# New orders of the same operations on four engines, with new users of the PSUM banks

## The reference

```
def local_ffn(x):                    # called twice, 2 layers each
    for l in range(2):
        h = shift_token(x)
        q, k, v = split(h @ wqkv[l])           # 8 heads of 64
        q, k = l2norm(q) * qs, l2norm(k) * ks  # then rotary with a scale by position
        o = local_attention(q, k, v)           # windows of 64, each looks at itself and the one before
        x = x + o @ wo[l]
        h = layernorm(shift_token(x)) * g + b
        a, gate = split(h @ w1[l] + b1[l])     # 341 each
        x = x + (a * gelu(gate)) @ w2[l] + b2[l]
    return x
x = x + 0.5 * local_ffn(layernorm(x))
x = x + causal_attention(layernorm(x))         # one head of 128, 1024 x 1024
x = x + 0.5 * local_ffn(layernorm(x))
```

## Time and profile before

| | us |
|---|---|
| median of 3 runs (lowest, highest) | 2623.74 (2619.52, 2624.07) |
| span of the profiled execution | 2623.2 |
| PE busy in it | 2558.0 |
| DVE, ACT, POOL busy | 2376.0, 2346.8, 2056.4 |

### The profile page before, as it was taken

The page is one execution under the profiler, slowest core; times in us unless marked ns, Lnnn a source line. Parts: engine busy times, 40 slices in busy tenths (PEclk is TensorE's granted clock), DMA queues, the critical chain, the costliest instruction groups (busy, mean ns, idle before and its releaser), DMA issues.

```text
span 2623.2 us, 80275 instructions
## 1 busy us (share of the span) xinstructions
PE 2558.0 (98%) x29132; PEld 2063.6 (79%) x29132; DVE 2376.0 (91%) x6206; ACT 2346.8 (89%) x7379; POOL 2056.4 (78%) x2185
## 2 busy tenths in 40 slices
PE   5999999999999999998999999999999999999998
PEld 4778777877788888886997777778777788888876
DVE  7999999999999999996888999999998999999995
ACT  5999999999999999995555999999999999999996
POOL 7999999988887877872104999999988888787873
PEclk8999999999999999999999999999999999999999
DMA  4121111111111111110000111111111111111110
GB/s 105 44 51 31 28 38 31 28 28 39 24 32 28 28 42 26 32 28 8 9 1 11 32 28 32 26 38 32 29 24 39 28 32 40 30 40 36 36 40 26
DMA packets 63810, 83.95 MB, mean 32 GB/s; under 512 B 11538, under 2 KB 30652, under 8 KB 63420
## 3 DMA queue, kind: packets, MB, share of 16 engines
q1 hardware_dynamic: 63420, 78.82, 13.1%
HBM read 11.67 MB, written 4.19 MB: 6 GB/s over the span
## 4 chain that ended last, share of the span: by engine, by line
PE 83%; POOL 6%; DVE 5%; ACT 4%; issue 2%; SPq 0%; DMA 0%; ACTq 0%; POOLq 0%; DVEq 0%
PE PS L678 8%; PE PS L662 8%; PE PS L628 7%; PE PS L652 7%; PE PS L619 6%; PE PS L742 6%; PE PS L621 6%; PE PS L620 6%; PE PS L723 4%; PE PS L725 3%; PE PS L724 3%; PE PS L644 3%; PE PS L690 2%; PE PS L853 2%; PE PS L692 2%
## 5 line engine op out<-in xcount | busy, mean ns | idle before, releaser
L4440 ACT ACTIVATE P<-PS,MX 128x128 f32<-128x128 f32 x2048 | 754.3, 430 | 2.1 <-DVE MX L2248 1.2
L5756 POOL TENSOR_TENSOR T<-T,SQ 128x512 f32<-128x512 f32 x512 | 652.1, 1284 | 115.3 <-DVE SQ L2209 111.7
L5792 POOL TENSOR_TENSOR P<-P,RI 128x512 f32<-128x512 f32 x512 | 527.8, 1042 | 73.8 <-DVE RI L2254 71.7
L4440 ACT ACTIVATION_READ_ACCUMULATOR P<-PS,MX 128x1 f32 x2048 | 535.6, 268 | 0.0
L5769 POOL TENSOR_TENSOR T<-T,RN 128x512 f32<-128x512 f32 x512 | 525.9, 1048 | 6.2 <-DVE RN L2242 3.8
L2190 DVE TENSOR_REDUCE SS<-SQ 128x8 f32<-128x512 f32 x512 | 343.8, 681 | 44.6 <-ACT SQ L4395 37.9
L4395 ACT ACTIVATE SQ<-PS 128x512 f32<-128x512 f32 x512 | 338.1, 662 | 45.9 <-PE PS L621 35.0
L619 PE MATMUL PS<-WH,YH 128*128 128x512 f32 x768 | 346.1, 451 | 6.9 <-POOL YL L5745 3.3
L2248 DVE TENSOR_REDUCE MX<-PS 128x4 f32<-128x512 f32 x512 | 345.8, 678 | 6.5 <-PE PS L652 6.3
L2209 DVE TENSOR_TENSOR SQ<-PS,TAB 128x512 f32<-128x512 f32 x512 | 349.1, 682 | 2.3
L2201 DVE TENSOR_TENSOR T<-PS,TAB 128x512 f32<-128x512 f32 x512 | 344.2, 682 | 7.1 <-PE PS L628 3.3
(11 more groups left out here) (155 smaller groups left out, 5938.4 us busy)
## 6 DMA issues: line engine op xcount, KB each, us to landing
VP<-VP SPq DMA_DIRECT2D x480, 128.0 KB, 2.3
out_dram<-X SPq DMA_DIRECT2D x16, 256.0 KB, 2.6
X<-in_L_attn_x_dram SPq DMA_DIRECT2D x7, 512.0 KB, 4.5
SG<-in_L_ffn_w_dram SPq DMA_DIRECT2D x5, 341.0 KB, 3.0
SG<-in_L_ffn_wqkv_dram SPq DMA_DIRECT2D x4, 384.0 KB, 3.4
SGQ<-in_L_ffn_wqkv_dram SPq DMA_DIRECT2D x4, 256.0 KB, 3.5
X<-in_table_dram SPq DMA_DIRECT2D x2, 512.0 KB, 6.5
P<-in_L_ffn_wo_dram SPq DMA_DIRECT2D x2, 256.0 KB, 3.2
```

What stands on the lines that cost most here:

```text
L4440: ins = act.activation(P[:, g, p, :], PS[:, b, 128 * p:128 * p + 128], ACT.Exp, bias=MX[:, g, p:p + 1], accum_out=SM[:, g, p:p + 1])
L5756: pool.tensor_tensor(T1[:, k, :], T1[:, k, :], SQ[:, (2 * n + 1 - x) % 3, :], ALU.add).then_inc(added[x], 1)
L5792: pool.tensor_tensor(P[:, g], P[:, g], RI[:, g, :].unsqueeze(2).broadcast_to([128, NPAIR, 128]), ALU.mult).then_inc(p_scaled, 1)
```

## The change

No operation is added, removed or changed in shape. All four lists are replaced; the rounds begin at 4 and 36 (before 9 and 41), since the lists before them are now short, and end at 32 and 64. The users of the banks are new, the banks of the attention too. The copies of the next layer's weights stand in calls of their own (`stage_qk`, `stage_v`, `rest_of_qk`, `rest_of_v`) and no longer inside `square`, `split_y`, `rotate_add` and `normalise_qk`. DVE takes the statistics of chunks 64 to 68 during the attention.

```diff
-ROUNDS = {0: (9, 32), 1: (41, 63)}
+ROUNDS = {0: (4, 32), 1: (36, 64)}
 ROTA = [
-    [("W2", 4), ("TK1", 3), ("O0", 4), ("V1", 2), ("TK0", 2), ("S0", 2), ("P2", 3), ("G0", 3)],
-    [("Q0", 2), ("YR", 3), ("TQ0", 2), ("K1", 1), ("O1", 3), ("NR", 1)],
...
+    [("TQ0", 3), ("TK1", 3), ("YT", 4), ("K0", 1), ("TQ0", 2), ("S0", 2), ("G1", 3)],
+    [("S2", 4), ("V1", 3), ("NR", 2), ("Q0", 1), ("TQ1", 2), ("WO", 2)],
...
-A_SCORE, A_TURN, A_OUT, A_IN = (0, 2), (4, 5), 6, 7
+A_SCORE, A_TURN, A_OUT, A_IN = (6, 3), (0, 2), 1, 5
```

The begin of DVE:

```diff
             y0_up(0)
+            ln_stats(2)
+            ln_aggregate(2)
+            ln_eps(2)
+            ln_stats(3)
             y0_up(1)
-            ln_stats(2)
+            ln_aggregate(3)
+            ln_eps(3)
+            ln_stats(4)
             sum_squares(0, 0, K)
```

More of the change, by code:

```diff
@@ L944, in first_steps @@
-            turn_back(0)
+            scores(4, 0)
+            turn_p(3, 1)
             project(5, 1, K)
-            turn(4, 1, K)
-            scores(4, 0)
-            project(5, 1, Q)
-            turn_p(3, 1)
+            turn(4, 1, Q)
+            turn_ln(6)
+            turn_p(3, 2)
+            to_gate(0, 0)
             wo(2)
-            project(5, 0, V)
-            turn(4, 1, Q)
-            turn_p(3, 2)
             turn_p(3, 3)
+            to_gate(0, 1)
             values(3, 0)
@@ L994, in first_steps @@
-            turn(6, 0, K)
-            turn(6, 1, K)
-            project(7, 1, K)
-            scores(6, 0)
-            turn_p(5, 1)
-            wo(4)
-            project(7, 0, V)
-            turn(6, 1, Q)
-            turn_p(5, 2)
-            turn_p(5, 3)
-            values(5, 0)
-            values(5, 1)
-            to_gate(1, 0)
-            to_gate(1, 1)
-            to_gate(1, 2)
-            turn_ln(8)
-            scores(6, 1)
-            wo(5)
-            to_up(1, 0)
-            to_up(1, 1)
@@ L1014, in first_steps @@
-            project(7, 1, V)
-            to_up(1, 2)
-            project(8, 0, K)
-            project(8, 0, Q)
-            down(1)
-            turn(7, 0, Q)
-            turn(7, 0, K)
-            turn_ln(9)
-            turn_p(6, 0)
-            turn_p(6, 1)
-            project(8, 1, K)
-            turn_p(6, 2)
-            turn(7, 1, K)
-            scores(7, 0)
-            turn_p(6, 3)
-            turn_rows(2)
-            turn(7, 1, Q)
-            project(8, 1, Q)
-            values(6, 0)
@@ L1052, in first_steps @@
-            turn_p(7, 3)
-            values(7, 0)
-            values(7, 1)
-            to_gate(2, 0)
-            to_gate(2, 1)
-            to_gate(2, 2)
-            turn_ln(10)
-            scores(8, 1)
-            wo(7)
-            to_up(2, 0)
-            to_up(2, 1)
-            project(9, 1, V)
-            to_up(2, 2)
-            project(10, 0, K)
-            project(10, 0, Q)
-            down(2)
-            turn(9, 0, Q)
-            turn(9, 0, K)
-            turn_ln(11)
-            turn_p(8, 0)
@@ L1146, in first_steps @@
-            wo(10)
-            project(13, 0, V)
-            turn(12, 1, Q)
-            turn_p(11, 2)
-            turn_p(11, 3)
-            values(11, 0)
-            values(11, 1)
-            to_gate(4, 0)
-            to_gate(4, 1)
-            to_gate(4, 2)
-            turn_ln(14)
-            scores(12, 1)
-            wo(11)
-            to_up(4, 0)
-            to_up(4, 1)
-            project(13, 1, V)
-            to_up(4, 2)
-            project(14, 0, K)
-            project(14, 0, Q)
@@ L3264, in into_attention @@
             a_add(0, 2)
+            ln_stats(TURN)
             a_copy_p(0, 4)
@@ new lines, in local @@
+                split_o(t - 5, 1)
+                gelu(s - 4, 1)
+                split_y(t - 2, 0)
+                y0_down(t - 1)
+                gelu(s - 4, 2)
+                round_w1(s - 3)
+                exp_rows(t - 4, 1)
+                square(t - 2, 0, K)
+                copy_v(t - 3, 0)
+                copy_k(t - 3, 0)
+                copy_q(t - 3, 0)
+                split_y(t - 2, 1)
+                square(t - 2, 0, Q)
+                exp_rows(t - 4, 2)
+                exp_rows(t - 4, 3)
@@ L4989, in into_attention, with attention @@
+                y0_down(t)
+                copy_q(t - 2, 1)
+                square(t - 1, 1, Q)
+                stage_qk(s)
+                copy_p(t - 3, 2)
+                copy_p(t - 3, 3)
+                exp_rows(t - 2, 0)
+                gelu(s - 3, 0)
+                split_o(t - 3, 0)
+        def attention():
+            split_o(TURN - 5, 1)
+            gelu(PAIRS - 4, 1)
+            split_y(TURN - 2, 0)
+            gelu(PAIRS - 4, 2)
             exp_rows(TURN - 4, 1)
-            split_o(TURN - 5, 0)
+            square(TURN - 2, 0, K)
+            copy_k(TURN - 3, 0)
@@ new lines, in local @@
+                rest_of_y(t - 2, 0)
+                normalise_qk(t - 3, 0, K)
+                normalise_qk(t - 3, 0, Q)
+                rotate_add(t - 3, 1, Q)
+                rest_of_w1(s - 3)
+                ln_root(t)
+                normalise_qk(t - 3, 1, Q)
+                scale_p(t - 4, 0)
+                normalise_qk(t - 3, 1, K)
+                ln_rows(t)
+                rest_of_y(t - 2, 1)
+                rotate_add(t - 2, 0, K)
+                scale_p(t - 4, 1)
+                row_rstd(s - 3)
```

5077 lines of the change are left out of this document (1447 added, 3630 removed), and 201 rows, old and new, of tables (FIRST_USERS, LAST_USERS, ROTA).

## The result

The changed kernel takes 2675.6 us (median of 4 runs, 2674.12 to 2676.56) against 2623.9 us for the kernel before on the same chip: ratio 1.0201, 95% interval 1.0186 to 1.0215. It is 2% slower, outside the range of 2588 to 2640. The profiled run has a span of 2672.3 us, 49.1 more than before. One execution of one experiment (e13_notab2) ran almost throughout at a low granted clock and took 4190.07 us; it is left out of all comparisons, and that kernel was run again as e16_notab3.

The account below looks back on a forecast made before the run. PE was taken as the limit in the rounds, with DVE, ACT and POOL also nearly full. The terms -3 - 3 - 3 - 1 - 4 - 1 = -15 took 2623.7 to 2609 us, range 2588 to 2640.

Parts of the forecast that it names:

- Neighbours on PE: In the rounds: costs between adjacent PE operations change by -0.05 us a round, -3 us over 60 rounds.
- Waits in the rounds: From a chunk's last projection to its first turn: a quarter of 11 us of first-layer-round waits goes, -3 us.
- the 0.9 us of slack: First-layer rounds: 11.1 us of PE cover less the 10.2 us way from last projection to first turn.
- this term is 0: ACT's order in the rounds: changes between exp and gelu stay at 123, so no cost from table loads, 0.
- Rival A: In the rounds: the shortened way is late at turn(t-3, 0, K), so slower, 2629 to 2650 us; chance 0.20.
- The begin: Before the first down: first turn at about 38 us, gain of -3 us, bounds -12 and +5.
- if it loses the same 17: The begin: first down at 125 us if waits take 17 us as before, 108 if nothing waits.
- break-even: The begin: a first down at 120 us would neither gain nor lose, as 4 us of work moved behind it.
- The clock: In the begin: the idle gap is as long, so the same loss from a lower granted clock, later; 0.
- Into the attention: Before the last values: to_gate and to_up fill 3.2 idle us but were cover behind it; -1 us, between -4 and +3.
- The end: End of the kernel: same exchange of fill and cover round the last values; -1 us, between -4 and +3.
- Out of the attention: After the attention: POOL is the bound, earlier statistics let it start sooner; -4 us, between -7 and 0.

Follow-up runs that it names:

- e13_notab2: Changed kernel without the second layer's tables, four small reduces in their place; ratio 1.0178, one execution at a low granted clock 4190.07 us.
- e16: Changed kernel without the second layer's tables, four small reduces in their place, run again; 2668.61 us, ratio 1.0173.
- e1: Changed kernel with less ACT work in the rounds: copy_p copies only 128 of 512 columns; 2662.28 us, ratio 1.0152.
- e3: Changed kernel with round_w1 moved later on ACT, behind copy_v, and rest_of_w1 behind row_rstd on POOL; 2667.66 us, ratio 1.0175.
- b2: Kernel before with round_w1 moved earlier on ACT, straight behind the last gelu of the pair; 2631.35 us, ratio 1.0026.
- e4: Changed kernel with own banks for Q1 and V0 of the first chunk, in the begin and after the attention; 2674.6 us, ratio 1.0200.
- e14: Changed kernel with own banks for Q1, V0 and also NR of the first chunk, in the begin and after the attention; 2679.04 us, ratio 1.0210.
- e7: Changed kernel with chunk 0's sums and root ahead of later statistics on DVE, and rest_of_y ahead of ln_rows on POOL; 2677.59 us, ratio 1.0202.
- e11: Changed kernel with own banks for Q1 and V0, and the first turn of K ahead of the next chunk's two Q projections; 2681.18 us, ratio 1.0220.
- e9: Changed kernel with the step into the attention back in the old order on PE, ACT and DVE to match; 2677.21 us, ratio 1.0201.
- e17: Changed kernel with two K projections moved behind the last two groups of values of the attention; 2676.12 us, ratio 1.0201.
- e2: Changed kernel with the second gelu ahead of the second split_o in ACT's order of the rounds; 2682.95 us, ratio 1.0232.
- e5: Changed kernel with the second layer's tables built one chunk later and one rotate_cos ahead of a sum_squares on DVE; 2678.01 us, ratio 1.0203.
- e12: Changed kernel with all three to_up ahead of wo on PE, and two gelu earlier on ACT; 2681.19 us, ratio 1.0217.
- e10: Changed kernel with the second layer's four table operations on 64 columns in place of 512; 2676.35 us, ratio 1.0196.
- b1: Kernel before with the second layer's four table operations on 64 columns in place of 512; 2621.25 us, ratio 0.9989.

## Why the prediction was wrong

*Neighbours on PE* (-0.05 us a round, -3, between -0.3 and +0.2 a round). With less work for ACT (e1) a YT round is within 0.05 to 0.14 us of the old one: inside the bounds, not on the side forecast, and not told apart from a rest of the wait.

*Waits in the rounds* (-3). This step failed twice. It took the 0.45 us by which an LT round is longer for waits that could go; but the LT round came out at 36.85 again, so this order won none of it (what it is, no run shows; less work for ACT did not change it either, 36.86 in e1). And it checked one way only, from `project(t - 1, 1, K)` to `turn(t - 3, 0, K)`. That way held: PE has no listed wait there, though the 0.9 us of slack was never measured. What was late was a way I had dismissed with "this term is 0": ACT's list. I had counted its table loads (124 in both kernels) and not whether the 21 us of its work from `copy_p` to the second `gelu` still fit beside PE's work between the same two points. They miss by 0.48 us a round, and only where `turn_ln` isn't there as cover. Rival A had the right kind of cause, at the wrong place and in the wrong rounds.

*The layer boundaries* were not in the sum at all. One conditional step moved from where its wait was already met to behind `gelu(s - 4, 2)`: 7.6 us, by e3, with b2 as its reverse. The rest of the 12.5, 4.9 us, is about the YT rounds' own wait in the same stretch: e1 took 5.9 us off the two boundaries.

*The begin* (-3). The first `turn` came at 37.19 as forecast (38), the first `down` at 129.90 and not 120. The step that failed is "if it loses the same 17": with the 70 us of work that the prediction counts behind the first `turn`, it lost 129.90 - 37.19 - 70 = 22.7. And -3 had been chosen although the sum with the same loss already stood at 125, 5 us over break-even. The list's shorter ways no longer cover a pause of DVE, which is also longer here (7.2 us against 4.5): 5.4 us of the 11.8 (e16). The other 6 us are not settled. They are not the shared banks (e4, e14), nor the order of statistics and sums (e7), nor PE's order round the first `turn` (e11).

*The clock* was put at 0, "the same loss, later". It was not the same: the granted clock's mean over the first 70 us is 0.78 against 0.88, and it fell behind the attention too, where it had not. In the begin its share lies inside the 5.4 and the 6 us above, behind the attention it is 1 to 2 us.

*Into the attention* (-1). The bounds named this loss, up to +3: the groups put ahead of the last `values` had been cover behind them. It was 4.2 us, and that cause is not shown: putting them back (e9) gave nothing sure. ACT's wait of the YT rounds is not in it either, since e1 has 84.4 us here. *The end* (-1): +0.7, inside its bounds.

*Out of the attention* (-4). The term took POOL for the bound. POOL was relieved for the first 20 us as forecast, and nothing was gained: PE waited 4.03 us for DVE to free bank 2. Of the 9.4 us the banks explain 1 and the clock 1 to 2; e17 and e11 excluded the position of two projections and of the first turn. Some 6 us stay open.

Together, e1, e3 and e16 took 13.3, 7.9 and 7.0 us away, each alone; e1 and e3 overlap at the boundaries, and no run has all three. By the table, of the 49 us some 20 have no cause shown: 6 in the begin, 4 into the attention, 6 behind it, the rest of the YT rounds and the end. The YT rounds and the layer boundaries are the largest part, 22.8 us. The time lies above even rival A's 2629 to 2650, which had neither the boundaries nor the losses into and out of the attention.

## What to carry to other kernels

When every engine is nearly full, judge a new order by each engine's list between each pair of its meetings with the bound engine, not by the one way that was shortened: sum the work in it and compare it with the bound engine's work between the same two points. Treat steps that act once in many rounds (a weight's rounding) as orders of their own: ask what they wait for at the new place and who is queued behind. And a removed wait in a full stretch mostly comes back one step later: of the eleven repairs tried here (e2 to e5, e7 to e9, e11, e12, e14, e17) only e3 made the kernel clearly faster. Last, look at an edit's own rows before its time is read: e10 and b1 left out seven eighths of an operation and most of its duration stayed.

## What the runs showed of the hardware

*An operation of DVE that reads two operands from SBUF can be held over several operations of POOL.* In e10 two operations of 64 columns took 4.73 us beside four `normalise_qk` of POOL; two more of the same, with POOL in other work, took 0.63. It need not be so: in b1 the same operations beside three `normalise_qk` took 1.28 and 1.48 us for two, about one operation of POOL for each pair. A reduce of the same 64 columns, one operand, took 0.35 for two, and POOL's own operations in e10 kept their length (4.04 us for four, 1.05 each in the earlier trace rows). The Trainium skill says in "SBUF — State Buffer", section "Who interferes with whom", that a DVE instruction with two SBUF inputs contends with a GpSimd instruction that reads SBUF, and that the order of issue decides who blocks. The traces agree: in e10 POOL was at work when DVE came, and DVE was held; in the kernel before DVE's first table operation started 0.15 us ahead of POOL's run, and POOL's three took 4.31 us and not the 3.05 of b1. They add that DVE was held over four of POOL's instructions in e10 and over about one in b1; what decides between the two, no run shows.

*A low granted clock can last while PE is busy.* In the trace of e13_notab2 the granted clock stayed at 0.55, between the two levels of 1.2 and 2.4 GHz and near the lower, though PE was busy for 58.89 of 60 us and then for 400 of 400 (stretch, length, PE, PEld, DVE, ACT, POOL, granted clock, DMA):

```profile
40.00:100.00 60.00, 58.89 (x481) 42.60 (x480) 41.59 (x111) 38.71 (x132) 46.33 (x50) 0.55 0.14 34
100.00:500.00 400.00, 400.00 (x2975) 273.84 (x2975) 241.18 (x644) 252.66 (x769) 227.65 (x244) 0.55 0.10 23
```

Ahead of it PE had waited 3.69 and 6.11 us. In e16, the same kernel, PE waited 4.28 and 6.11 us, and the clock is back at 1.00 from 60 us on. What decides it, these runs don't show.
